# Second batch's values from split operands in one-pass products, with the splitting on GpSimd

## The reference

```python
q = split_heads(layernorm(x) @ w_q.T + b_q)      # 2 x 16 heads x 256 x 16
k = split_heads(ctx @ w_k.T + b_k)               # 2 x 16 heads x 4096 x 16
v = split_heads(ctx @ w_v.T + b_v)
scores = where(mask, -inf, q @ k.T / 4)
x = x + (softmax(scores) @ v) @ w_o.T + b_o
# then retention and experts, each on layernorm(x)
```

## Time and profile before

| what | us |
|---|---|
| median of 3 runs | 205.86 |
| the profiled execution's own time | 204.96 |
| its span, first to last instruction | 203.1 |
| PE busy | 193.9 |
| DVE busy | 140.0 |
| ACT busy | 108.2 |
| POOL busy | 74.7 |

### The profile page before, as it was taken

The page is one execution under the profiler, slowest core; times in us unless marked ns, Lnnn a source line. Parts: engine busy times, 40 slices in busy tenths (PEclk is TensorE's granted clock), DMA queues, the critical chain, the costliest instruction groups (busy, mean ns, idle before and its releaser), DMA issues.

```text
span 203.1 us, 5924 instructions
## 1 busy us (share of the span) xinstructions
PE 193.9 (95%) x2446; PEld 134.5 (66%) x2446; DVE 140.0 (69%) x269; ACT 108.2 (53%) x230; POOL 74.7 (37%) x96
## 2 busy tenths in 40 slices
PE   8998999989999999999999999999999999999991
PEld 8566654555576767666666656476777888878780
DVE  3482568997388286688888627289676485996893
ACT  3136575759588386788888996244416333201200
POOL 8506695556191241079998331001003013010000
PEclk9999999999999999999999999999999999999998
DMA  5969966338209679066000000000000000000011
GB/s 165 299 189 258 329 161 162 90 85 230 50 5 241 135 207 362 20 217 204 5 5 5 3 0 3 0 3 0 0 0 2 3 0 2 0 5 26 26 32 36
DMA packets 15828, 18.10 MB, mean 89 GB/s; under 512 B 2657, under 2 KB 14897, under 8 KB 15793
## 3 DMA queue, kind: packets, MB, share of 16 engines
q1 hardware_dynamic: 14496, 17.30, 29.1%
q10 hardware_dynamic: 1296, 0.34, 0.8%
HBM read 9.81 MB, written 0.52 MB: 51 GB/s over the span
## 4 chain that ended last, share of the span: by engine, by line
PE 79%; DVE 8%; SPq 4%; ACT 3%; issue 2%; DMA 1%; POOL 0%; DVEq 0%; ACTq 0%; POOLq 0%
PE bank L919 11%; PE bank L1014 11%; PE bank L996 11%; PE bank L876 5%; PE bank L862 4%; DVE cneg L1849 4%; PE bank L1214 3%; PE bank L1064 3%; PE bank L1103 3%; PE bank L1238 3%; PE bank L1107 3%; PE bank L1240 3%; PE bank L1239 3%; PE bank L809 3%; PE bank L1104 3%
## 5 line engine op out<-in xcount | busy, mean ns | idle before, releaser
L1849 DVE TENSOR_REDUCE cneg<-bank 128x1 f32<-128x896 f32 x64 | 67.9, 1088 | 25.1 <-PE bank L919 24.8
L1526 ACT ACTIVATE prob<-bank 128x512 f32<-128x512 f32 x112 | 64.3, 600 | 13.2 <-PE bank L996 11.8
L996 PE MATMUL bank<-qstack,kstack 100*32 100x256 bf16 x896 | 45.0, 273 | 0.8 <-ACT prob L1526 0.5
L919 PE MATMUL bank<-kstack,qstack 97*32 97x448 bf16 x512 | 37.5, 354 | 1.6 <-DVE cneg L1849 0.9
L996 PEld LDWEIGHTS bank<-qstack,kstack 100*32 100x32 bf16 x896 | 24.4, 95 | 18.9 <-ACT prob L1526 4.1
L1014 PE MATMUL bank<-prob,vals 128*32 128x256 f32 x448 | 35.6, 381 | 0.0
L604 POOL TENSOR_TENSOR nw<-nw,halves 128x2 f32<-128x2 f32 (+1 forms) x10 | 8.3, 825 | 63.6 <-DVE nw L1730 45.1
L919 PEld LDWEIGHTS bank<-kstack,qstack 97*32 97x32 bf16 x512 | 13.6, 96 | 7.7 <-DVE cneg L1849 3.5
L1014 PEld LDWEIGHTS bank<-prob,vals 128*32 128x32 f32 x448 | 13.5, 109 | 4.5 <-issue 2.9
L1238 PE MATMUL bank<-exp_high,xn_high 128*128 128x512 f32 (+1 forms) x36 | 14.3, 397 | 0.0
L2095 DVE SCALAR_TENSOR_TENSOR x_in<-bank,nwts,x_in 128x256 f32<-128x256 f32 x28 | 13.5, 482 | 0.8
(11 more groups left out here) (186 smaller groups left out, 322.1 us busy)
## 6 DMA issues: line engine op xcount, KB each, us to landing
kstack<-kpart SPq DMA_DIRECT2D x21, 224.0 KB
w_late<-in_w_ret SPq DMA_DIRECT2D x1, 1536.0 KB, 8.7
mask_all<-in_mask SPq DMA_DIRECT2D x2, 512.0 KB, 4.5
ctxT<-in_w_exp SPq DMA_DIRECT2D x1, 1024.0 KB, 5.3
kpart<-in_w_exp SPq DMA_DIRECT2D x1, 1024.0 KB, 8.9
ctxT<-in_ctxT SPq DMA_DIRECT2D x2, 448.0 KB, 5.0
ctxT<-in_ctxT SPq DMA_DIRECT2D x1, 896.0 KB, 7.9
qstack<-acc SPq DMA_DIRECT2D x12, 64.0 KB, 4.1
```

Source lines behind the costliest of these rows:

```text
L919: mm = pe.matmul(out[j4:j4 + COLS, :], qstack[0:MROW + 1, h, b, qt * P + j4:qt * P + j4 + COLS], kstack[0:MROW + 1, b, h, half_ * HC:(half ...
L996: mm = pe.matmul(out[j4:j4 + COLS, hh * NQ:(hh + 1) * NQ], kstack[0:KROWS, b, h, kt * P + j4:kt * P + j4 + COLS], qstack[0:KROWS, h, b, :] ...
L1526: act.activation(prob[:, n % PROBS, :], bank[:, c.score_bank(u, jj), :], ACT.Exp).then_inc(c["prob_ready"], 1)
L1849: dve.tensor_reduce(cneg[:, st % 2, i:i + 1], bank[:, pair:pair + 2, 0:HC], AXXY, ALU.max, negate=True).then_inc(c["max_read"], 1)
```

## The change

The values of the second batch are no longer formed from fp32 operands. The context and the weights are each written as a high part (rounded to fp32r) and a low part (the rest), and each fp32 product becomes three one-pass products: high x high, high x low, low x high. POOL forms the parts: `split_context` (high part of the context, high and low part of the weights) goes ahead of `cut_maxima(1)`, and `split_context_rest` (low part of the context, written over the context itself, hence after the keys that read it) between `cut_maxima(2)` and `keys_cut(3)`. PE waits for all five. The counter `split` now has these five steps ahead of the ones it had.

```diff
+CTX_PARTS = 3 + KIN
-SPLIT_RET = 3
+SPLIT_RET = CTX_PARTS + 3
...
+            def split_context():
+                pool.wait_ge(*only.at("v_evac", NVP))
+                pool.wait_ge(*only.key("k_taken", 2))
+                pool.wait_ge(s["q_taken"], 3)
+                pool.wait_ge(*only.at("ctx_loaded1", 16))
+                pool.tensor_copy(ctx_high[:, :, :], ctxT[:, 1, :, :]).then_inc(s["split"], 1)
+                pool.tensor_copy(wv_high[:, :, :], wv[:, :, :]).then_inc(s["split"], 1)
+                pool.wait_ge(s["split"], 2)
+                pool.tensor_tensor(wv_low[:, :, :], wv[:, :, :], wv_high[:, :, :].bitcast(F32), ALU.subtract).then_inc(s["split"], 1)
+
+            def split_context_rest():
+                pool.wait_ge(*only.key("k_taken", 3))
+                for i in range(KIN):
+                    pool.tensor_tensor(ctx_low[:, i, :], ctxT[:, 1, i, :], ctx_high[:, i, :].bitcast(F32), ALU.subtract).then_inc(s["split"], 1)
...
             with pool.If(fast > 0):
                 pool.wait_ge(s["q_cut"], 3)
+                split_context()
                 cut_maxima(1)
                 keys_cut(only, 2)
                 cut_maxima(2)
+                split_context_rest()
                 keys_cut(only, 3)
...
+            def split_values(blocks, out):
+                pe.wait_ge(s["split"], CTX_PARTS)
+                for k in blocks:
+                    some, keys_ = out[:, (k - blocks[0]) * D:(k - blocks[0] + 1) * D], slice(k * P, (k + 1) * P)
+                    for i in range(KIN):
+                        pe.matmul(some, ctx_high[:, i, keys_], wv_high[:, i, :], start=(i == 0), stop=False)
+                        pe.matmul(some, ctx_high[:, i, keys_], wv_low[:, i, :], start=False, stop=False)
+                        mm = pe.matmul(some, ctx_low[:, i, keys_], wv_high[:, i, :], start=False, stop=(i == KIN - 1))
+                mm.then_inc(only["v_ready"], 1)
```

More of the change, by code:

```diff
@@ L134 @@
 BROWS, BLOW = 40, 32
-SPLIT_RET = 3
-SPLIT_EXPERT = (6, 9)
-SPLIT_ALL = 14
+CTX_PARTS = 3 + KIN
+SPLIT_RET = CTX_PARTS + 3
+SPLIT_EXPERT = (CTX_PARTS + 6, CTX_PARTS + 9)
+SPLIT_ALL = CTX_PARTS + 14
 PER = {"k_ready": 8, "k_hi": 4, "k_rest": 4, "k_taken": 4, "k_mid": 4, "k_cut": 4, "v_ready": NVP + 2, "v_evac": NVP + 2,
@@ L377, in build @@
         gate_parts = sb("gate_parts", [P, KIN, 2, NE], F32R)
+        ctx_high = sb_over("ctxT", 0, "ctx_high", [P, KIN, CH])
+        ctx_low = sb_over("ctxT", 4 * KIN * CH, "ctx_low", [P, KIN, CH])
+        wv_high = sb_over("wq", 0, "wv_high", [P, KIN, D])
+        wv_low = sb_over("wv", 0, "wv_low", [P, KIN, D])
         xn_high = sb_over("wq", 0, "xn_high", [P, KIN, TT * P])
@@ L707, in split_late @@
                 pool.tensor_copy(ret_high[:, :, :], w_ret[:, :, :]).then_inc(s["split"], 1)
-                pool.wait_ge(s["split"], 1)
+                pool.wait_ge(s["split"], CTX_PARTS + 1)
                 def ret_rest(c):
@@ L801, in _ @@
                 stream_and_bias()
+                pool.sem_inc(s["split"], CTX_PARTS)
                 split_late(lambda i: None)
@@ L886, in values @@
                 value_blocks(c, 0, range(2 * n, min(2 * n + 2, KB)), bank[:, c.value_bank(n), :])
+            def split_values(blocks, out):
[7 more added lines that the diff above has]
+                mm.then_inc(only["v_ready"], 1)
             def later_values(c, n):
                 pair = take_pair(c, "v", n)
-                value_blocks(c, 1, range(4 * n, min(4 * n + 4, KB)), bank[:, pair:pair + 2, :].rearrange("p b k -> p (b k)"))
+                out = bank[:, pair:pair + 2, :].rearrange("p b k -> p (b k)")
+                blocks = range(4 * n, min(4 * n + 4, KB))
+                if c.loop:
+                    value_blocks(c, 1, blocks, out)
+                else:
+                    split_values(blocks, out)
             def max_tile(c, m):
```

## The result

The changed kernel takes 209.57 us, the median of 4 runs (207.5 to 210.6), against 205.9 before; the ratio is 1.0165 (95% interval 1.0085 to 1.0246). Beside the experiments it took 210.02 (6 runs), ratio 1.014 (1.0075 to 1.0204). The forecast was 206.1 with 204.3 to 207.8 around it: the change costs about 3.6 us where I gave it 0.3. The spans of the profiled executions are 206.77 and 203.14 us, 3.63 apart, so they hold the whole of it. Ratios leave out disturbed executions; medians are over all runs.

The account below looks back on a forecast made before the run. PE's time bounds the kernel, with SP's queue behind POOL a second path to step 21. Step 21 comes 0.88 us late, the second piece returns 0.58: +0.30 on 205.86, so 206.1 us, range 204.3 to 207.8.

Parts of the forecast that it names:

- the right place: Start of stage 3 (step 21), between the two pieces of values, where PE waits for the DMA that brings `mrows`.
- from issue to PE it takes 2.05 us: Stage 3's rows: SP's DMA issue at 73.09 to PE's start at 75.14, carried over unchanged to the new kernel.
- PE's part: Values on PE: one-pass products take 2.95 and 2.21 us, saving 0.70 and 0.58, together 1.28 us.
- POOL's first part, at no cost: Ahead of stage 1's maxima: 3.6 us (at most 4.4) fits POOL's idle time; 0.79 us room against at most 0.6 delay.
- POOL's low half: Ahead of `keys_cut(3)`: two subtractions of 2.09 us, 4.18 in all, ending 5.1 us before PE asks for it.
- The rival's 2.57 each: Slower case's price for each of POOL's two low-half subtractions, ending 0.96 us later than forecast; chance 12%.
- SP: SP's queue behind POOL: `bo_row` issued 1.65 us late, the lag then taken as 1.03, `load_rows(3)` issued at 73.97.
- The hold at `wo`: SP's `wo` issue, 1.69 us: lag 0.41 if the hold goes, 1.65 if it stays whole; 1.03 taken.
- The sum: Step 21 starts 0.88 us late, the second piece takes back 0.58: +0.30 us net, 206.1 us.
- Slower: Rival at step 21: costlier low half, wait at `wo` kept, lag 2.61, net +1.9 us, 207.8; chance 12%.
- The queue recovers: Rival at SP: its long issues shrink, no lag, step 21 starts 0.15 earlier, net -0.73, 205.1 us; chance 28%.
- the growing wait for `mrows`: Sign ahead of step 21: PE's wait grows from 0.45 to about 2 us.

Follow-up runs that it names:

- c_low_after_keys: Changed kernel with POOL forming the context's low half behind `keys_cut(3)` instead of ahead of it; 205.56 us against 205.56 for the kernel before, ratio 1.0004.
- c_decay_after: Changed kernel with the decay table's 768 KB load moved behind the rows of stage 3; 206.0 us against 205.56 for the kernel before, ratio 1.0022.
- c_kept_busy: Changed kernel with 12 useless fp32 products on PE just ahead of the wait for stage 3's rows; 207.07 us, ratio 1.0067 to the kernel before.
- c_fp32_values: Changed kernel with POOL's work kept but values formed as fp32 products of the high parts alone; 210.26 us over 10 runs, ratio 1.0105 from three.
- c_again: The changed kernel once more, no edit, beside the experiments; 210.02 us (6 runs), ratio 1.014 to the kernel before.
- c_half_busy: Changed kernel with 5 useless products on PE ahead of the wait for stage 3's rows; 208.55 us, ratio 1.0101 to the kernel before.
- c_rows_mid: Changed kernel with stage 3's rows issued just ahead of the decay table, `gn` and `gb_row`; 204.82 us against 205.56 for the kernel before, ratio 0.9962.
- c_experts_later: Changed kernel with stage 3's rows ahead of the decay table and the experts' 2 MB loads behind stage 5's rows; one run, 213.29 us.

## Why the prediction was wrong

The prediction had the right place and the right chain. It failed in "from issue to PE it takes 2.05 us", which it carried over to a new state of the queue and which became 3.32, and it had no term for what a long wait does to PE's clock, which cost 1.66 more.

- *PE's part.* Forecast 2.95 and 2.21 us, saving 1.28. Measured 3.00 and 2.29, saving 0.65 + 0.50 = 1.15. The one-pass products start 0.117 us apart, and the fp32 ones are two instructions 0.216 apart, so three products replace 0.432 us by 0.351. By the estimate from the Trainium skill ("FP8 and Floating Point Precision", section "TensorE Precision Notes") the saving would have been 1.61; the trace disagrees: an fp32 product costs 3.7 of the one-pass ones, not four, and the pieces save 18%.
- *POOL's first part, at no cost.* Right: 1.68, 0.61 and 1.27 against 1.66, 0.6 and 1.19; the maxima were split at 42.11.
- *POOL's low half.* Right: 4.16 against 4.18, and PE had 5 us of room. The rival's 2.57 each did not occur.
- *SP.* In the changed kernel's own time (0.25 less), `bo_row` came 1.59 late against 1.65. The hold at `wo` stayed whole, 1.64, where I had let 0.62 of it go. Further down the table's own issue grew from 0.35 to 0.72 and the one of `gn` shrank from 1.29 to 0.41, so 0.51 came back there. So the rows were issued 0.91 late against 0.88 forecast: right, by two errors that cancel.
- *Issue to PE: the failed step.* "From issue to PE it takes 2.05 us" was taken as a constant. It became 3.32. The shrunken hold at `gn` is the other side of it: before, 2.36 us lay between the table's issue and the rows' issue, after 1.71, so the rows stood closer behind the same data. `c_low_after_keys` has 2.64 between the two, and a transit of 2.04; `c_decay_after`, with the table behind, 2.03; the transits of 3.3 to 4.5 all belong to distances under 2.0. The sizes of the DMA packets in the traces tell the two loads apart, and show where the time goes (the table moves as 128 packets of 6144 bytes, the rows as 16 of 512):

  | run | table's packets started 1.34 us after the rows' issue | rows' packets, first start and last end after the issue | issue to PE |
  |---|---|---|---|
  | `c_decay_after` | none, it is behind | 1.35, 1.50 | 2.03 |
  | `c_low_after_keys` | 127 | 1.35, 1.51 | 2.04 |
  | before | 121 | 1.35, 1.51 | 2.05 |
  | after | 73 | 2.30, 2.90 | 3.32 |
  | `c_kept_busy` | 80 | 2.15, 2.32 | 3.34 |
  | `c_fp32_values` | 110 | 1.81, 3.89 | 4.29 |
  | `c_again` | 76 | 2.15, 4.05 | 4.45 |
  | `c_half_busy` | 84 | 2.31, 4.07 | 4.47 |

  Before, the table's data had all but left when the rows could start. After, its first packet came 1.68 us later (73.38 instead of 71.70), the rows' issue only 0.66, and the rows' packets began when the table's last ones did, at 76.1. In the last three runs 8, 8 and 12 of the 16 packets moved only 1.4 us or more behind the others; what held those stays open. The Trainium skill ("DMA: Bandwidth & Descriptors", section "Two DMAs through the same engine are not ordered") says that descriptors of one queue start in order on each DMA engine; by that rule the small DMA starts behind the table's. The traces agree; the size is the runs'.
- *The clock: a term that was missing.* I forecast a wait of 2.0 us and priced it at 2.0. It was 3.3, and the clock fell for 3.4 us, which cost 1.66. `c_kept_busy` removes exactly that from the stretch behind the wait.
- *The sum.* +0.30 forecast, +0.03 at SP, +1.27 for the transit, +1.66 for the clock, +0.08 for the smaller saving of the second piece (that of the first is lost in the wait) and +0.5 in stage 4, less the 0.25 at the start, is 3.59 against 3.63. The forecast with the longer transit alone, 0.30 + 1.27 = 1.57 over 205.9, would give the 207.5 of the two runs whose clock did not fall; as they have no profile, that may be chance.
- *The rivals.* "Slower" had the right place and 1.9 us, near those two runs, but by the wrong price (the low half's), so the nearness is luck. "The queue recovers" happened in part, at `gn`, and gave nothing back.
- *The signs.* Of those I named, the growing wait for `mrows` was right in kind: from 0.45 to 3.3, not 2. The issue of the rows came at 74.0 in the forecast's own time, as named. No rival named a longer transit or a fall of the clock, and the range ended 1.8 us below the result.

## What to carry to other kernels

An operation added to an idle engine is priced at the queue that starts from its result: here 4.2 us on an engine busy for 37% reached PE through eighteen DMA issues on SP. A small DMA that somebody waits for belongs ahead of bulk loads, since its transit depends on the data in front; moving one line of SP's list made this change a gain of 0.7 us instead of a loss of 3.6. And a wait of 3 us on PE can cost more than 3 us: here the clock fell behind it in 8 of 10 runs, and 1.66 us went with that in the profiled one; so a forecast that ends in a new wait of that size needs a second case for that.

## What the runs showed of the hardware

- The granted clock stayed up over idle times of PE, by its weight loads, of 1.88 us (`c_decay_after`) and 2.09 us (`c_rows_mid`) and fell for 3.4 us, the same length each time, behind ones of 2.71, 3.28, 3.83 and 4.6 us in the profiled executions; in `c_experts_later` it was low for 6.8 us after PE had stood 6.5 us. By their mean clock, other runs of the same kernels had no such fall, so a mean over runs hides more than one case.
- An 8 KB DMA took 2.01 to 2.05 us from issue to its reader where the 768 KB were behind it or issued 2.36 us or more ahead, and 3.3, 4.3 and 4.5 us where they were issued 1.6 to 2.0 us ahead. Its packets started 1.33 to 1.35 us after the issue when the way was free, and otherwise among the last of the 768 KB's, 1.8 to 2.3 us after it.
- SP's own issues are held up in one place or another (`wo` 1.6 to 1.7, `gn` 0.41 to 1.71 us): with the table's load moved away, `gn` behind it was held 1.08 us instead of 0.41.
- PE stood 0.7 to 2.1 us in stage 4 with nothing to wait for that the profile shows, in seven of the twelve profiled kernels that loaded 2 MB then, but not in the kernel before; it did not in the one kernel without that load at that time.
